# Three stages instead of a chunk loop: projections in fp16 parts, then the gated layer of all chunks, then attention

## What is computed

```
xn = layernorm(x)
s  = attention(xn)          # 32 heads of 16, causal, ALiBi slopes, biases, output projection
g  = silu(ffn(xn))          # gated layer: silu(gate) * up, then down
out = x + s * g
```

## Time and profile before

| | |
|---|---|
| median of three runs | 937.5 us (936.05 to 940.85) |
| the profiled execution's own time | 936.63 us |
| its span | 934.8 us |
| mean granted clock of TensorE | 0.975 of full |
| PE busy | 836.0 us (89%), 6144 matmuls |
| VectorE, ScalarE, GpSimd busy | 615.7, 495.0, 114.7 us |
| HBM read and written | 44.86 and 29.63 MB |

### The profile page before, as it was taken

The page is one execution under the profiler, slowest core; times in us unless marked ns, Lnnn a source line. Parts: engine busy times, 40 slices in busy tenths (PEclk is TensorE's granted clock), DMA queues, the critical chain, the costliest instruction groups (busy, mean ns, idle before and its releaser), DMA issues.

```text
span 934.8 us, 16870 instructions
## 1 busy us (share of the span) xinstructions
PE 836.0 (89%) x6144; PEld 442.4 (47%) x6144; DVE 615.7 (66%) x1453; ACT 495.0 (53%) x642; POOL 114.7 (12%) x127
## 2 busy tenths in 40 slices
PE   4498999999999998999899998999999989997976
PEld 3384456745774575333334343333343433433654
DVE  5478542354136412782898988888888888882398
ACT  3565642144214321221777777777777777778310
POOL 2030321131213121220000000000000000000042
PEclk8598999999999999999999999999999999999988
DMA  7431003200320022500022212122222111253667
GB/s 188 109 112 60 9 12 114 102 1 23 112 90 0 22 79 99 124 1 35 23 72 61 70 49 58 52 68 71 72 60 72 48 53 54 71 175 106 220 208 284
DMA packets 67600, 75.74 MB, mean 81 GB/s; under 512 B 26550, under 2 KB 38838, under 8 KB 67528
## 3 DMA queue, kind: packets, MB, share of 16 engines
q1 hardware_dynamic: 67416, 74.51, 25.7%
q0 software_dynamic: 112, 0.27, 0.1%
HBM read 44.86 MB, written 29.63 MB: 80 GB/s over the span
## 4 chain that ended last, share of the span: by engine, by line
PE 32%; DVE 10%; issue 8%; DMA 5%; ACT 4%; SPq 2%; ACTq 0%; DVEq 0%
PE psum L1362 11%; PE psum L1324 8%; DVE mx L1217 7%; PE psum L1341 4%; ACT probs L1168 4%; DMA o_scr<-osum 2%; PE psum L1328 2%; PE psum L267 2%; PE psum L268 1%; DMA r_scr<-den 1%; DMA probs<-in_L_attn_x 1%; PE psum L278 1%; PE psum L279 1%; PE psum L1350 1%; SPq L1084 1%
## 5 line engine op out<-in xcount | busy, mean ns | idle before, releaser
L1168 ACT ACTIVATE probs<-psum,exp_scale 128x1024 f32<-128x1024 f32 (+1 forms) x256 | 244.8, 1008 | 71.4 <-PE psum L1350 40.8
L1217 DVE TENSOR_REDUCE mx<-psum 128x1 f32<-128x512 f32 (+2 forms) x368 | 217.6, 648 | 25.6 <-PE psum L1328 16.0
L1324 PE MATMUL psum<-QKs 51*128 51x512 f16 (+3 forms) x768 | 180.5, 330 | 22.9 <-DVE mx L1213 10.2
L1213 DVE CUSTOM_DVE_ANT_0 mshown<-psum,ahead 128x384 bf16<-128x384 f32 (+2 forms) x288 | 155.5, 583 | 20.6 <-PE psum L1324 16.8
L1341 PE MATMUL psum<-QKs 53*128 53x512 f16 (+3 forms) x768 | 147.3, 328 | 16.1 <-ACT probs L1168 13.8
L267 PE MATMUL psum<-X,MG 128*128 128x512 f16 (+1 forms) x352 | 135.3, 384 | 4.2 <-PEq L341 3.7
L268 PE MATMUL psum<-X,MG 128*128 128x512 f16 (+1 forms) x352 | 134.9, 383 | 0.0
L1362 PE MATMUL psum<-probs,Vs 128*32 128x512 f32 (+3 forms) x1152 | 127.0, 524 | 0.2 <-ACT osum L1179 0.2
L1324 PEld LDWEIGHTS psum<-QKs 51*128 51x128 f16 x768 | 50.6, 93 | 160.7 <-DVE mx L1217 71.7
L295 ACT ACTIVATE hid<-psum,sig_scale 128x512 f32<-128x512 f32 (+1 forms) x44 | 30.2, 687 | 138.4 <-PE psum L268 138.4
L1168 ACT ACTIVATE X<-psum,exp_scale 128x1024 f32<-128x1024 f32 x64 | 67.9, 1116 | 16.5 <-PE psum L1350 16.1
(11 more groups left out here) (147 smaller groups left out, 1129.9 us busy)
## 6 DMA issues: line engine op xcount, KB each, us to landing
o_scr<-osum SPq DMA_DIRECT2D x32, 256.0 KB, 2.9
QKs<-q_scr SPq DMA_DIRECT2D x96, 64.0 KB
QKs<-k_scr SPq DMA_DIRECT2D x96, 64.0 KB
q_scr<-qk_stage SPq DMA_DIRECT2D x16, 256.0 KB, 2.2
k_scr<-qk_stage SPq DMA_DIRECT2D x16, 256.0 KB, 2.2
v_scr<-v_stage SPq DMA_DIRECT2D x16, 256.0 KB, 2.0
g_scr<-g_stage SPq DMA_DIRECT2D x16, 256.0 KB, 2.0
Vs<-v_scr SPq DMA_DIRECT2D x16, 256.0 KB
```

What stands on the lines that cost most here:

```text
L1168: nc.scalar.activation(probs[n % PSLOTS][:, 2 * pair:2 * pair + 2, 0:COLS[n]], s_bank[pair][:, :, 0:COLS[n]], ACT.Exp, scale=exp_scale[:, ...
L1213: nc.vector.tensor_tensor_reduce(out=mshown[at % 2][:, 0:keys], in0=m_bank[bank][:, 0:keys], in1=ahead[:, CH - keys:], scale=1.0, scalar=L ...
L1217: nc.vector.tensor_reduce(dst, m_bank[bank][:, 0:n * keys].rearrange("p (n k) -> p n k", n=n), AX.X, ALU.max).then_inc(max_read, 1)
L1324: last = nc.tensor.matmul(tile[:, hh, :], Qs[s][rows, pair + hh, qb * P:(qb + 1) * P], Ks[s][rows, pair + hh, k0:k0 + keys], start=(hh == ...
```

## The change

- **Projections for all four chunks first**, with both weights (W16, OW) and x (X16) as two fp16 parts. A power-of-two scale for each weight group is worked out on the chip from its sum of squares (squares, sum_squares, scale_of). x is split once instead of twice, so two operations for each tile instead of four.
- **The start.** PE waits for the four tiles of the query weight and for chunk 0's x only. The key weight follows behind the first tile, value and output weight beside tiles of chunks 0 and 1. The second query tile needs bank and weights that wait for the scale of the key weight.
- **Side work in the projection stage.** Ternary values beside chunks 1 and 2, place_down and place_gate_up beside chunks 2 and 3, all six of ScalarE's place_down beside chunk 2, transposes of down beside chunk 3. Layer norm of chunk c+1 lies beside chunk c, and its split x beside c's value tiles.
- **The gated layer of all chunks** in the order 2, 3, 0, 1 as one stage, with five banks; chunks 0 and 1 of X16 are stored (x_scr) and loaded again. The first 52 maximum tiles lie beside its second half, one behind each of the last 52 tiles. Sigmoid(z) is made from Tanh(z/2).
- **One block, no hardware loops**, no barrier; queue SP issues the loads of the first quads at the end of the projections. Attention's order is kept. In the tail the output projection is in fp16 parts, and finish uses scalar_tensor_tensor with a scale from a [128,1] tile.

The core of the diff:

```diff
-                pe.wait_ge(wl_done, NWT)
...
-                pe_gated(pe, 0, bank_of, free, beside)
-                with pe.Fori(1, LAST) as c:
-                    qk(c)
-                    v(c)
-                    pe_gated(pe, c, bank_of, free, beside_of(c))
-                qk(LAST)
-                v(LAST)
...
+            for kt in range(KT):
+                transpose_weight(kt)
+            sum_squares(0)
+            for kt in range(KT):
+                transpose_x(0, kt)
+            for kt in range(KT):
+                transpose_weight(KT + kt)
+
+            for c in range(NCH):
+                for m in range(NQK):
+                    query_key(c, m)
+                    if c == 0 and m < 2:
+                        sum_squares(1 + m)
+                    if c == 1 and m == 0:
+                        sum_squares(3)
+                    if c < 2 and 2 - c <= m < 2 - c + KT:
+                        transpose_weight((2 + c) * KT + m - 2 + c)
+                    if c == 1 and m == 6:
+                        pe.wait_ge(asum_done, 4)
+                        nc.tensor.matmul(side(SIDE_MEAN)[:, 0:3], ones[:], asum[:], start=True, stop=True).then_inc(mean_ready, 1)
+                    if c == 2 and 1 <= m <= NTT:
+                        transpose_ternary(m - 1)
+                    if c == 3 and m >= 1:
+                        transpose_down(m - 1)
+                for t in range(TT):
+                    value(c, t)
+                    if c + 1 == NCH:
+                        transpose_down(NQK - 1 + t)
+                    elif t == 0:
+                        transpose_x(c + 1, 0)
+                        transpose_x(c + 1, 1)
+                    elif t < TT - 1:
+                        transpose_x(c + 1, t + 1)
```

query_key, its wait, and the ring:

```diff
+            def free(g):
+
+                if g >= RING:
+                    pe.wait_ge(evac_done, g - RING + 1)
+                elif g == 2:
+                    pe.wait_ge(scale_ready, 2)
+                else:
+                    pe.wait_ge(wl_done, (4, 5, 0, 6, 7, 8)[g])
+
+            def query_key(c, m):
+                cols = slice(m * P, (m + 1) * P)
+                bank = ring_bank(c * TILES + m)
+                if m == 0:
+                    pe.wait_ge(xl_done, (c + 1) * KT)
+                if c == 0 and m == KT:
+                    pe.wait_ge(wl_done, 2 * KT)
+                free(c * TILES + m)
```

ScalarE and VectorE beside the projections:

```diff
+            for c in range(NCH):
+                for m in range(NQK):
+                    evacuate(c, m)
+                    if c < 2 and 2 - c <= m < 2 - c + KT:
+                        high_weight((2 + c) * KT + m - 2 + c)
+                    if c == 2 and 1 <= m <= NTT:
+                        copy_ternary(m - 1)
+                    if c == 2 and m == NTT + 1:
+                        act.wait_ge(tern_dn, 1)
+                    if c == 2 and m > NTT:
+                        place_down(m - NTT - 1)
...
+                for t in range(TT):
+                    if c + 1 < NCH:
+                        split_x(c + 1, t)
+                    if c == 2 and t < ACT_DOWN - 3:
+                        place_down(3 + t)
...
+                for t in range(TT):
+                    values(c, t)
+                    if c + 1 < NCH:
+                        split_x(c + 1, t)
+                    if c == 1 and t < 2:
+                        ternary_gate_up(t)
```

The order of the gated layer with the first maxima, which PE, VectorE, ScalarE and SP all follow:

```diff
+F_FIRST = 2 * FTILES
...
+    for n, tile in enumerate(tiles):
+        order.append(("ffn", *tile))
+        due = max(n + 1 - F_FIRST, 0) * len(early) // (len(tiles) - F_FIRST)
+        order += [("maximum", *x) for x in early[given:due]]
+        given = max(given, due)
```

More of the change, by code:

```diff
@@ new lines, in program, with take @@
+        at = [0]
+        def take(n):
+            at[0] += n
+            return room[:, at[0] - n:at[0]]
+        MG = take(N_MG).bitcast(f16).rearrange("p (t w h) -> p t w h", t=KT, w=2)
+        MD = take(N_MD).bitcast(f16).rearrange("p (t d) -> p t d", t=HT)
+        hid = [take(CH) for i in range(NSIG)]
+        g_stage = [take(CH) for i in range(2)]
+        shared = take(2 * N_HH)
+        HHs = shared[:, 0:N_HH].bitcast(f16).rearrange("p (t n) -> p t n", t=HT)
+        HLs = shared[:, N_HH:].bitcast(f16).rearrange("p (t n) -> p t n", t=HT)
@@ new lines, in program @@
+        c_rows = alloc(one, "c_rows", [P, (ROWS_MAX - ROWS_QK) * PAIRS * S // P], f16)
+        asum = alloc(one, "asum", [P, 3], f32)
+        mean = alloc(one, "mean", [P, 3], f32)
+        half = alloc(one, "half", [P, 3], f32)
+        nhalf = alloc(one, "nhalf", [P, 3], f32)
+        gu_scale = alloc(one, "gu_scale", [P, 1], f32)
+        dump = [QKs[i // 2][:, i % 2].rearrange("p h t -> p (h t)").bitcast(bf16) for i in range(4)]
+        one.close()
+        two = ExitStack()
+        top.enter_context(two)
@@ L226, in program @@
         xl_done = sem("xl_done")
+        x_kept = [sem(f"x_kept{i}") for i in range(2)]
+        squared = sem("squared")
+        sum_done = sem("sum_done")
+        scale_step = sem("scale_step")
+        scale_ready = sem("scale_ready")
+        c_ready = sem("c_ready")
+        c_stored = sem("c_stored")
         wt_done = sem("wt_done")
@@ L402, in dve_normalise, with _, link, normalise_x @@
+            copy_out(QUADS - 1, 1, ENDS[1])
+            for c in range(1, NCH):
+                high_attention(c)
+        @block.vector
+        def _(dve):
+            scaled = [0]
+            meant = [0]
+            def link(ins, signal, count):
+                count[0] += 1
+                ins.then_inc(signal, 1)
+                dve.wait_ge(signal, count[0])
+            def normalise_x(c, stage):
                 base = c * LN_STEPS
                 if stage == 0:
-                    first = isinstance(c, int) and c == 0
@@ new lines, in _ @@
+            invert(0)
+            invert(1)
+            dve.wait_ge(bo_loaded, 16)
+            normalise(0)
+            low(0)
+            normalise(1)
+            invert(2)
+            low(1)
+            invert(3)
+            for c in range(2):
+                dve.wait_ge(o_stored[c], QUADS * 16 + 16)
+            for c in range(NCH):
+                finish(c)
+                if c + 2 < NCH:
+                    normalise(c + 2)
+                    low(c + 2)
+        @block.tensor
```

1901 lines of the change are left out of this document (925 added, 976 removed).

## The result

The changed kernel takes 926.6 us (median of 4 runs, 924.0 to 927.9) where the kernel before, run beside it, takes 939.0 (936.1 to 940.9). The ratio is 0.987, with a 95% interval of 0.984 to 0.990: 1.3% faster where 2.0% was forecast. The profiled span is 926.1 us against 934.8, so 8.7 of the 18.0 us of the sum came between these two executions. The medians differ by 12.5 us: of the changed kernel the slowest of the four executions was profiled (927.9), of the kernel before one near its fastest (936.6).

A forecast was written before the change was run, and what follows sets the result against it. PE work or pauses were taken as the bound between head and attention. Terms of -6.3, -11.5, -9.4, -3.8, +8.7, +3.1 and +1.2 sum to -18.0 us, taking the span from 934.8 to 916.8; forecast 919 us, range 905 to 932.

The forecast's parts named there:

- pitch: Projections: fp16 matmuls spaced 0.2158 us instead of 0.2267 for fp32r, -6.3 us.
- head: Start of the kernel: projection stream as if started at 27.9 us instead of 44.35, less work moved into it, -11.5 us.
- pauses of chunk 0's gated layer, barrier: PE's waits around chunk 0's gated layer (-9.4 us) and the barrier between the blocks (-3.8 us) go away.
- new waits in the projections: Changes of chunk: PE waits for x splits, 4.0 us for chunks 0 and 1, the rest after chunk 2; +8.7 us.
- first maxima: Second half of gated layer: lone maximum tiles cost more ways in and out than clusters, less waits saved; +3.1 us.
- attention: Attention stage keeps its order and its 427 us; term of 0 shared with the gated layer, bounds -1 to +3.
- tail: Output projection's finish on VectorE: scalar_tensor_tensor with a scale from a tile costs slightly more per operation, +1.2 us.
- the forecast's band: Whole kernel at 911 to 927 us: PE stays the bound, head and pauses go, chunk changes give some back; 55%.
- rival 3: Chunks 2 and 3 of the projections: side work exposed, late layer norm holds PE's x transposes; 927 to 933 us, 13%.
- The third chunk change: End of chunk 2: ScalarE's last split is late behind six place_down, so PE waits 4.6 us, 0.1 more for drain.
- rival 2: Whole kernel better: ScalarE keeps up (4.7 us less), lone maxima cost no more than clustered ones (7 less); 900 to 911, 17%.
- Rival 5: Projections: query/key stores pace the stream and make the kernel slower, about 945 us; 6%.

The follow-up runs named there:

- run 1: Changed kernel with chunk 0's and 1's split-x stores behind their chunk's own stores and the output-weight load behind chunk 0's third store: 920.5 us, ratio 0.981.
- run 2: Changed kernel with VectorE taking each layer-norm step in chunk 2 ahead of that slot's placing of gate and up weights: 927.0 us, ratio 0.986.
- run 7: Changed kernel with two of VectorE's three gate/up placings moved from chunk 2 to chunk 3: 924.7 us, ratio 0.985.
- run 8: Changed kernel with four edits: stores first, two placings moved to chunk 3, split ahead of the last value tile, first maxima in threes: 908.6 us, ratio 0.967.
- run 10: Version of run 8 with VectorE doing chunk 3's layer norm earlier, ahead of its placings, and ScalarE's root one slot earlier: 906.4 us, ratio 0.964.
- run 11: Version of run 8 with ScalarE's operations placing the down weight spread over more slots, VectorE unchanged: 907.9 us, ratio 0.965.
- run 12: Version of run 8 with both the earlier layer norm on VectorE and ScalarE's spread placings: 900.9 us, ratio 0.959.
- s4_clusters: Changed kernel with the first maxima given three after each third tile instead of one after each: 913.9 us, ratio 0.973.
- run 6: Version with clusters of three, with the last four first maxima kept until after the last gated tile: 913.8 us, ratio 0.973.

## Why the prediction was right in direction and too large in size

The forecast was -18.0 us; -8.7 came in the profiled pair and -12.5 in the medians. Term by term, from the profiled pair:

| term | forecast | measured | from |
|---|---|---|---|
| pitch | -6.3 | as forecast | query tiles of 12 products in 2.59 us, 0.2158 each |
| head | -11.5 | -10.2 | stream as if started at 29.2, not 27.9 |
| pauses of chunk 0's gated layer, barrier | -13.2 | as forecast | no pause but the last between 151 and 436 us |
| new waits in the projections | +8.7 | +16.9 | 3 x 1.84 (with the drain) + 5.0 + 3.6 + 2.8 |
| first maxima | +3.1 | +4.4 | stage 251.96 where the sum had 250.7 (1056 x 0.2158 + 19.7 + 3.1) |
| attention | 0 | +1.9 | 428.86 against 427.01 |
| tail | +1.2 | -2.0 | 60.75 against 62.78 |

The measured column sums to -8.5. All that was off but the tail fell on the dear side; the tail came out 3.2 us under its forecast, which was luck, as said below, and it helped to keep the result within the forecast's band.

**The step that failed is the term of the new waits**, mis-sized by 8.2 us, at three places.

*Stores in chunk 0, 5.0 us* (about 2 of them above what the other profiles had, an estimate from chunk 0's lengths in run 1). The prediction counted nothing: the loads ahead of the first store would be "through at about 32", and "without this cover the PSUM ring of six tiles (15 us) hides it". SP was through at 33.5 and then issued two more megabytes before the first store, at 35.33. And the ring hides nothing, because PE does not only fill it: between tiles it transposes weights, and their low halves stand in VectorE's queue behind the cast that waits. Run 1 shows it. The Trainium skill ("DMA: Bandwidth & Descriptors", Queues, rings and completion order) says that descriptors of one issuing queue are consumed in ring order on each DMA engine. The landing of 9.4 us behind the megabytes and 2.9 without them agrees.

*Chunk 2, 6.4 us.* This is rival 3's mechanism (13%), of which the forecast had no part. I had summed ScalarE's work by slot for this chunk, but VectorE's only over a whole chunk "before". Runs 2, 7 and 8 show that order, or VectorE's load alone, does not mend it; runs 10 to 12 show that two queues have to be mended: VectorE's late statistics hold ScalarE at the root, and ScalarE's placings then come late and the splits with them. Either queue alone leaves the other as the limit. Of VectorE's lateness 1.87 us are a wait for a store, at 127.52, ahead of the placing and the norm; a wait of 1.8 us or more for a store is in chunk 2 of every version, and no run took it away.

*The third chunk change, 2.9 us too dear.* 4.7 us was forecast for ScalarE being late, 1.84 came. The mechanism exists (3.88 us in runs 7 and 8) but lay under the late norm.

**First maxima.** Their size in the sum held within 1.3 us, but "lone maxima cost no more than clustered ones", which rival 2 priced at 7 us, was the wrong question: against clusters that no wait holds up the lone ones cost 10.6 us more. I took the 0.31 and 0.32 of the earlier trace rows for a price of each visit and never asked what two products in one visit cost. The row there, `388.10 0.60 ... x2`, hides it: its second product starts 0.21 us after the first. In the next cluster, at 391.08, the first two start together (both within 0.39 us), and all three take 0.91 us from gated product to gated product. The Trainium skill states it ("TensorEngine Tiling (Array Packing)", Key Properties): a change of tiling mode drains the engine, and different tiles can load weights and multiply in parallel. Both are in the traces: 0.1 us on either side of a visit, and two starts at 323.67. The page speaks against lone maxima, and the prediction should have weighed it.

**Head.** The second query tile came at 30.45, after 29.2 was forecast, with 3.13 us of idle before it as forecast. The first came at 24.23 instead of 20.1. The fourth piece of the query weight landed at 13.04, 1.7 us after I had its square finished, and the eight pairs of splits (four of x, four of the weight) with the x transposes between them took 6.5 us instead of 5.2. Most of the first tile's delay was absorbed, as it then ran at full speed. This was read from the trace, and no run tested it.

**Attention and tail.** Attention's 1.9 us lie in its first 13.5 us, with 10 us at the slow clock where the kernel before has 5 us at 0.67; s4_clusters has 0.67 too (427.1 us). In the thirteen profiles the same attention took 426.8 to 429.1 us. When the clock falls here, and for how long, varied between versions with the same order of work, and what decides it stays open; keeping products back did not prevent it (run 6). Of the tail's 2.0 us, 0.9 lie between the first product of the output projection and the end of VectorE's last operation, 58.3 us against 59.2 before. In these thirteen profiles, in which its code is the same, that took 58.0 to 61.5 us, so the kernel before lies within the scatter. The other 1.1 us lie behind VectorE's last operation (2.4 us against 3.6). The forecast's rise of 0.05 us per operation shows (0.74 us a piece where 0.69 stood), and is lost in that scatter. As forecast, the operation beside GpSimd stayed dearer than alone: 1.19 us against 0.75. (The 0.9 us that the prediction puts on the two-input form in chunk 0 are 0.6 by the pace that it names: 2.42 less 1360/512 x 0.69. No term uses them.)

**Rival 5**, stores as the pace, did not come: VectorE waited for a store five times in the changed kernel, 8.13 us in chunk 0 and at most 1.97 after it, and PE's chunks 1 and 3 show no pause for them. So its sign of a wrong prediction, a store named as what VectorE waits for, did appear, and gave PE a pause of its own at one place only.

## What to carry to other kernels

When side work is moved beside another engine's stream, sum every queue slot by slot, with who waits for whom, and not over the stage: here a root of 0.2 us tied two queues together, and over the two chunks concerned mending one gave 2.8 us, the other 4.7, and both 9.0. Ask of each instruction that may wait for a DMA what is queued behind it on its engine; a ring of buffers covers only what goes through the ring. Products that use half of the array's rows belong in pairs on different halves, next to each other: scattered one by one, 52 of them cost 10.3 us more than in twos and 10.6 more than in threes.

## What the runs showed of the hardware that I had not expected

- Two fp16 products of 51 rows and 512 columns on different row halves start in the same instant and cost 0.22 us together, plus 0.1 us on either side where 128-row products are the neighbours.
- The first 256 KB stores took 9.4 us to land behind 2 MB issued within 2 us ahead of them, and 2.9 without those; before it was 2.1 to 3.0.
- A pause of 3.6 us is followed by 5 us at half the clock (0.50), which adds 2.8 us; pauses of 1.7 us at the chunk changes had no such effect (clock 1.00 in chunk 1, which lies between two).
- VectorE's sum with epsilon, 128x4 elements and one input tile, took 1.86 us at 7.90 in the head, while GpSimd's memsets of V ran (8.29 to 9.73); the same operation took 0.15 at 125.49, and 0.35 in the head of the kernel before. The thirteen profiles agree: in the three where it started by 7.7 it took 0.28 to 0.50 us, in the ten where it started between 7.9 and 8.6 it took 1.20 to 1.86 us and ended at 9.75 to 9.78, right behind the memsets (9.72 to 9.76). No run moved the memsets; the fourth square of the weight, which landed at 13.04, came later anyway.
